# A gated recurrent mixer and its ternary FFN on one Trainium2 core: every engine's order in the mix stage is rewritten, the DMA issues of ScalarE go to SyncE and GpSimd

## The reference, cut to what matters

```
bc = einsum('bti,oi->bto', value, W_bc).reshape(B, T, H=32, 4, N=32)
bc = bc / (sqrt(sum(bc*bc, -1)) + EPS)
Bz, Bx, Cz, Cx = bc[...,0,:], bc[...,1,:], bc[...,2,:], bc[...,3,:]
def step(z, s):                      # for each of 512 positions
    S = 1 / (1 + dt*k + dt*dt*A)
    z = S * (z - dt*A*s + dt*Bz*u)
    s = s + dt*z + dt*Bx*u
    y = Cz . z + Cx . s
```

## Time and profile before

| | us |
|---|---|
| median of 3 runs | 2783.38 (2770.19 to 2786.92) |
| the profiled execution | 2786.88 |
| its span in the trace | 2785.2 |
| project / mix / ffn in the span | up to about 320 / 320 to 2466 / 2466 to 2785 |
| PE, DVE, ACT busy over the span | 81%, 67%, 42% |

### The profile page before, as it was taken

One profiled execution on the slowest core, in us unless ns is written; L12 is line 12 of the kernel. 1 busy time (PEld: TensorE's weight loads), 2 busy tenths in 40 slices (PEclk: granted clock), 3 DMA queues, 4 the chain that ended last, 5 costly groups with the idle time before them and its releaser, 6 DMA issues. The chain is left out here.

```text
span 2785.2 us, 56799 instructions
## 1 busy us (share of the span) xinstructions
PE 2266.9 (81%) x20514; PEld 1412.6 (51%) x20514; DVE 1869.4 (67%) x4268; ACT 1167.1 (42%) x2659; POOL 362.4 (13%) x540
## 2 busy tenths in 40 slices
PE   5655387989889898989898998989898997646886
PEld 2322133555555555555554555555555556545775
DVE  5655336867668776858676777668586777527775
ACT  3444233444526253534435353535445352313543
POOL 0000011111111111111111111111011110025210
PEclk9777688899889898889898898989888886557997
DMA  3444443334343434334443434243443433052320
GB/s 117 123 135 141 140 119 97 111 109 120 96 113 109 115 90 123 95 102 117 107 116 90 119 103 121 80 132 101 106 123 100 109 100 84 3 193 111 130 75 23
DMA packets 240313, 299.22 MB, mean 107 GB/s; under 512 B 127905, under 2 KB 144289, under 8 KB 231841
## 3 DMA queue, kind: packets, MB, share of 16 engines
q1 hardware_dynamic: 129248, 145.24, 17.5%
q10 hardware_dynamic: 93248, 112.51, 15.1%
q0 software_dynamic: 17536, 37.78, 5.0%
HBM read 240.85 MB, written 51.39 MB: 105 GB/s over the span
## 5 line engine op out<-in xcount | busy, mean ns | idle before, releaser
L642 PE MATMUL m_ps_a<-m_valT,m_w_bc 128*128 128x512 f32 x2048 | 1063.5, 672 | 67.0 <-DMA m_valT<-scratch_valT 32.1
L642 PEld LDWEIGHTS m_ps_a<-m_valT,m_w_bc 128*128 128x128 f32 x2048 | 426.3, 217 | 574.9 <-issue 565.4
L597 POOL DMA_DIRECT2D m_shear<-scratch_shear x512 | 277.1, 542 | 1831.5 <-DVE m_psi L1004 1617.1
L1000 DVE TENSOR_TENSOR m_prod<-m_psi,m_shear 128x128 f32<-128x128 f32 x1024 | 294.9, 288 | 38.7 <-ACT m_shear L771 14.0
L1004 DVE TENSOR_TENSOR m_psi<-m_psi,m_prod 128x128 f32<-128x128 f32 x1024 | 293.4, 287 | 17.2
L812 ACT ACTIVATE m_sq<-m_ps_a 128x512 f32<-128x512 f32 x256 | 153.2, 598 | 293.5 <-PE m_ps_a L642 235.1
L771 ACT ACTIVATE m_shear<-m_shear,m_A 128x64 f32<-128x64 f32 x512 | 135.8, 338 | 332.8 <-DMA m_shear<-scratch_shear 301.6
L698 PE MATMUL m_ps_g<-m_raw 32*64 32x64 f32 x8192 | 189.2, 253 | 69.1 <-DVE m_g L1108 61.3
L678 PEld LDWEIGHTS m_ps_k<-m_u,m_kT 64*128 64x128 f32 x1792 | 190.0, 197 | 67.7 <-ACT m_kT L838 39.7
L723 PE MATMUL m_ps_k<-m_raw,m_Xb 128*112 128x64 f32 x1024 | 177.2, 306 | 57.3 <-ACT m_Xb L856 57.3
L698 PEld LDWEIGHTS m_ps_g<-m_raw 32*64 32x64 f32 x8192 | 168.7, 163 | 96.3 <-issue 80.2
(11 more groups left out here) (146 smaller groups left out, 2975.8 us busy)
## 6 DMA issues: line engine op xcount, KB each, us to landing
m_scale<-scratch_norm SPq DMA_DIRECT2D x512, 128.0 KB
m_w_bc<-in_w_bcT ACTq DMA_DIRECT2D x252, 256.0 KB, 2.9
m_shear<-scratch_shear POOLq DMA_DIRECT2D x512, 64.0 KB, 2.7
m_det<-scratch_ab ACTq DMA_DIRECT2D x64, 256.0 KB, 5.9
scratch_gateT<-gate SPq DMA_DIRECT2D x8, 1024.0 KB, 3.9
scratch_valT<-val SPq DMA_DIRECT2D x8, 1024.0 KB, 4.5
scratch_svgT<-svg SPq DMA_DIRECT2D x8, 1024.0 KB, 5.8
scratch_u<-p_u SPq DMA_DIRECT2D x8, 1024.0 KB, 7.7
```

What stands on the lines that cost most here:

```text
L597: pool.dma_start(shear[h * N:(h + 1) * N, w % 2].rearrange("p k g t -> p k (g t)"), spread(src)).then_inc(into.sem, into.step)
L642: mm = pe.matmul(ps_a[j % 2].ap(), w_bc[:, j, kt, :], valT[:, kt, :], start=(kt == 0), stop=(kt == KI - 1))
L1000: dve.tensor_tensor(prod.ap().rearrange("p k g r -> p (k g) r"), psi_kt[of_half][:, :, t, :], window.unsqueeze(2).to_broadcast([P, 2 * HAL ...
```

## The change

- `LEAD` is 5 instead of 4: TensorE is one unit further ahead.
- TensorE, state part: before, `transposes`, unit, `state_terms`, unit, for each group (the fourth without the last unit). After, unit, `transposes`, unit, `state_terms`, so 8 units there instead of 7.
- TensorE, scores: half of a unit (two of its four weight tiles) is put behind each of the two bursts of scores, instead of a whole unit behind both. Between the outputs of a group and the scores of the next, there is one more unit; three units that stood behind the first group's scores and two that stood before the last outputs are spread out so.
- TensorE, `state_terms`: a semaphore increment on `narrow_next` ahead of it. Its matmuls stay as they are.
- ScalarE issues no more `valT`, `e_end`, `u`, `y` and `ab` DMAs. `ab` goes to GpSimd, all the others to SyncE, where a list for each half now orders them with the norm traffic. ScalarE keeps the loads of `w_bc`.
- ScalarE's order: logs of the determinants move from the start of a half to the end of the half before it, between window 9 and the third copy of `y`; the exponentials move ahead by one unit.
- VectorE's order: scaling of a group's inputs and outputs comes earlier by up to two steps, so that at the start of a half only keys are left of the current half; `queries` of the second group come before `states` (so the wait on `X_ready` goes from the second group's queries to the third's, as they share a buffer); the last mask comes before the keys of the next half instead of after it.

```diff
-    LEAD, PHASE = 4, UNITS // 2
+    LEAD, PHASE = 5, UNITS // 2
...
@@ sync
+                def norm_rows(b, group):
+                    sp.wait_ge(rows_ready.sem, rows_ready.at(b, group - 1))
+                    load_factor(b + group // HG, group % HG)
+                    compact_norms(b, group)
+                def input_scales(b, group):
+                    sp.wait_ge(rows_ready.sem, rows_ready.at(b, group))
+                    sp.dma_start(dram["norm"][group % 2]..., compact.ap()).then_inc(rows_stored.sem, rows_stored.step)
+                    sp.wait_ge(rows_stored.sem, rows_stored.at(b, group))
+                    sp.wait_ge(c_scaled.sem, c_scaled.at(b, group - 1))
+                    load_scales(group % 2, 0)
+                def output_scales(b, group):
+                    sp.wait_ge(b_scaled.sem, b_scaled.at(b, group))
+                    load_scales(group % 2, 1)
+                def store_y(b, group, more):
+                    sp.wait_ge(y_ready.sem, y_ready.at(b, group * 2 + 1))
+                    for h in range(HP):
+                        sp.dma_start(dram["yT"][b, group, h * DH:(h + 1) * DH, :],
+                                     y[h * N:h * N + DH, :]).then_inc(y_stored.sem, y_stored.step)
+                    if more:
+                        load_u(b, group + HALF)
...
+                    for half in range(2):
...
+                        if more:
+                            norm_rows(b, then)
+                            input_scales(b, then)
+                            load_e_end(b, half + 1)
+                            output_scales(b, then)
+                            norm_rows(b, then + 1)
+                            input_scales(b, then + 1)
+                            output_scales(b, then + 1)
+                            norm_rows(b, then + 2)
+                        if half == 0 and not last:
+                            sp.wait_ge(a_made.sem, a_made.at(b, UNITS - 1))
+                            load_valT(b + 1)
+                        store_y(b, first, more)
+                        if more:
+                            input_scales(b, then + 2)
+                            output_scales(b, then + 2)
+                            norm_rows(b, then + 3)
+                        store_y(b, first + 1, more)
+                        if more:
+                            input_scales(b, then + 3)
+                            output_scales(b, then + 3)
+                        store_y(b, first + 2, more)
+                        store_y(b, first + 3, more)
...
@@ gpsimd
+                            if w == NW and not (last and half):
+                                pool.wait_ge(det_used.sem, det_used.at(b, half))
+                                load_ab(b, half + 1)
...
@@ tensor
+                    pe.sem_inc(narrow_next, 1)
...
-                    product(b, unit, last)
+                        product(b, unit, last, pair * 2, pair * 2 + 2)
...
                         for i in range(HALF):
+                            products(b, unit, 1, last)
                             transposes(b, first + i)
-                            products(b, unit, 1, last)
+                            products(b, unit + 1, 1, last)
                             state_terms(b, first + i)
...
                         scores_and_unit(b, first, unit, last)
-                        products(b, unit + 1, 3, last)
+                        products(b, unit + 1, 1, last)
...
                             scores_and_unit(b, first + i, unit, last)
                             outputs(b, first + i - 1)
-                            unit += 1
-                        products(b, unit, 2, last)
-                        unit += 2
+                            products(b, unit + 1, 1, last)
+                            unit += 2
                         outputs(b, first + HALF - 1)
...
@@ scalar
                         copy_terms(b, first + 1)
+                        det_inverses(b, half)
                         evacuated(1)
...
                         block_states(b, first)
                         window(6)
                         evacuated(1)
+                        copy_y(b, first)
+                        block_states(b, first + 1)
                         window(7)
+                        evacuated(2)
                         window(8)
+                        copy_y(b, first + 1)
+                        block_states(b, first + 2)
                         evacuated(1)
                         window(9)
+                        if more:
+                            det_logs(b, half + 1)
+                        evacuated(1)
+                        copy_y(b, first + 2)
+                        block_states(b, first + 3)
+                        evacuated(1)
+                        copy_y(b, first + 3)
...
@@ vector, the order of a half after the change (then = the same group of the next half)
    keys(first+1); scales(then); keys(first+2); scale_inputs(then); det_sums; scale_outputs(then);
    keys(first+3); queries(first); queries(first+1); scales(then+1); coefficients; states; mask(first);
    scale_inputs(then+1); queries(first+2); mask(first+1); scale_outputs(then+1); scales(then+2);
    queries(first+3); scale_inputs(then+2); mask(first+2); scale_outputs(then+2); scales(then+3);
    advance(OF_PHASE); scale_inputs(then+3); mask(first+3); keys(then); scale_outputs(then+3)
```

More of the change, by code:

```diff
@@ new lines, in load_e_end, with load_u @@
+                def load_e_end(b, half):
+                    for h in range(HP):
+                        first = h * HG + half % 2 * HALF
+                        sp.dma_start(e_end[h * N:(h + 1) * N, half % 2 * HALF:half % 2 * HALF + HALF, :],
+                                       spread(dram["e_end"][b + half // 2, first:first + HALF])).then_inc(e_end_in.sem, e_end_in.step)
+                def load_u(b, group):
+                    g_ = group % HG
+                    of_group = slice(g_ * HP * DH, (g_ + 1) * HP * DH)
+                    into = u_in[group % HALF]
+                    sp.dma_start(u[:, group % HALF], dram["u"][b + group // HG][:, :, of_group]).then_inc(into.sem, into.step)
@@ new lines, in _ @@
+                load_valT(0)
+                load_e_end(0, 0)
+                for group in range(HALF):
+                    load_u(0, group)
+                for group in range(HALF):
+                    norm_rows(0, group)
+                    input_scales(0, group)
+                    output_scales(0, group)
+                def body(b, last):
+                    for half in range(2):
+                        more = not (last and half)
+                        first = half * HALF
+                        then = first + HALF
+                        if more:
[21 more added lines that the diff above has]
+                        store_y(b, first + 3, more)
@@ L587, in _, with load_ab @@
                 over_rows(sp, body)
+                sp.wait_ge(y_stored.sem, y_stored.at(B - 1, HG * HP - 1))
             @block.gpsimd
             def _(pool):
+                def load_ab(b, half):
+                    for h in range(HP):
+                        first = h * HG + half % 2 * HALF
+                        pool.dma_start(det[h * N:(h + 1) * N, :, :],
+                                       spread(dram["ab"][b + half // 2, first:first + HALF])).then_inc(ab_in.sem, ab_in.step)
@@ L807, in evacuate @@
                     act.wait_ge(a_made.sem, a_made.at(b, unit))
-                    if unit == UNITS - 1 and not last:
-                        load_valT(b + 1)
                     if j == 0 and unit:
@@ L824, in det_logs @@
                     for i in range(HALF):
-                        group = half * HALF + i
+                        group = half % 2 * HALF + i
                         ins = act.activation(det[:, i, :], det[:, i, :], ACT.Ln, bias=one[:, :], scale=A[:, group:group + 1])
@@ L881, in _ @@
                         scale_shear(0, 0, (unit + 1) // 2)
+                    if unit == 2:
+                        det_logs(0, 0)
                 scale_shear(0, 1, 0)
@@ L928, in body @@
                         copy_terms(b, first + 3)
-                        if more:
-                            load_e_end(b, half + 1)
                         window(5)
@@ L1212, in phase @@
                     queries(b, first + 3, advance)
+                    if more:
+                        scale_inputs(b, then + 2, advance)
                     mask(b, first + 2, advance)
                     if more:
-                        scale_inputs(b, then + 2, advance)
+                        scale_outputs(b, then + 2, advance)
                         scales(b, then + 3, advance)
                     advance(OF_PHASE)
-                    advance = stepping(b, half + 2, not last)
                     if more:
-                        keys(b, then, advance)
-                    if half:
-                        advance = stepping(b, half + 2, False)
```

(4 more changed lines are left out.)

116 lines of the change are left out of this document (29 added, 87 removed).

## The result

| | before | after |
|---|---|---|
| median, us | 2778.43 (2770.19 to 2786.92, 4 runs) | 2836.38 (2835.70 to 2846.56, 4 runs) |
| span of the profiled execution | 2785.2 | 2834.0 |

The changed kernel is slower: ratio 1.0209, 95% interval 1.0179 to 1.0240, 58 us. I had forecast 2748.

A forecast was written before the change was run, and what follows sets the result against it. The bound was a loop of dependences per half, T + C = 126.7 us, falling to 121.9; with valT 4 per row this saved 44, less 9 for prologue and last half: 2752 profiled, 2748 median, range 2650 to 2835.

The forecast's parts named there:

- T: Tail of the loop, from the last psi step to the next half's first `scales`: 30.6 us, forecast 29.6.
- C: Rest of the loop, from first `scales` to last psi step: 96.1 us, forecast 92.3.
- work in C: VectorE's work between first `scales` and last psi step: 73.3 us, plus 7.0 for moved keys and steps, 80.3.
- waits in C: VectorE's waits between first `scales` and last psi step: forecast 12 us per half, against 22.8.
- (d): Last part of T: y copy, SyncE's y stores and u, then factor and compact loads until landing: 10.4 us.
- the 9.65: VectorE's last listed wait in C, 9.65 us; to go, as the last compact loads follow an earlier scaling.
- valT: SyncE issues this load some 2.5 us after unit 31; TensorE waits 3 to 4: 4 per row, bounds 0 and 8.
- Row border: ScalarE's idle 8.58 us between rows: counted as nothing, or 5 per row if SyncE had such a stall.
- Prologue: Start of the kernel: 14 us longer, as the fourth group's input and output scaling precede the first keys.
- Table load: ScalarE's table switch, taken as 1.28 us without drain; the skill's 1.38 drain would make the sum 2769.
- The slower rival: SyncE becomes the bound: its waits for y copies delay third and fourth groups' scale loads; 2838 us, chance 0.21.
- Signs named beforehand: Right: compact waits from 281 to about 150 us; C wrong: `m_scale` waits far above 6 per half.

The follow-up runs named there:

- e6: Changed kernel, with ScalarE instead of SyncE issuing each half's last group's four y stores and u load: 2767.5 us.
- e2: Changed kernel, with ScalarE's logs of the next half's determinants ahead of shear window 9 instead of behind it: 2786.3 us.
- e1: Changed kernel, with GpSimd's 1 MB `ab` load held until the next half's third group's input scaling is done: 2788.0 us.
- e11: Changed kernel with the edits of e2 and e6, windows 2 and 3 behind the term copies, and the `ab` load held as in e1: 2714.6 us.
- e15: Changed kernel with the edits of e2 and e6, windows 2 and 3 behind the term copies, and ScalarE issuing `ab` ahead of window 8: 2686.3 us.
- e16: Changed kernel, with the last group's y stores and u load, and the `ab` load ahead of window 8, back on ScalarE: 2734.9 us.
- e9: Changed kernel, with whole units again three behind the first scores (one halved) and two ahead of the last outputs: 2970.9 us.
- e13: Changed kernel, with all four groups' y stores and u loads issued by ScalarE again: 2796.2 us.
- e3c: Changed kernel, with the next group's factor and compact loads ahead of SyncE's last y stores and u load, in first halves only: 2805.4 us.
- e14: Changed kernel, with shear windows 2 and 3 behind the copies of the first two groups' terms: 2839.0 us.

## Why the prediction was wrong, step by step

The two parts of the loop, averaged over 13 halves in the middle of either trace:

| | before | predicted | after |
|---|---|---|---|
| T | 31.7 | 29.6 | 30.8 |
| C | 95.6 | 92.3 | 99.3 |
| work in C | 73.5 | 80.3 | 81.0 |
| waits in C | 22.1 | 12 | 18.3 |

- **T** was sized well (1.2 off), part by part: from the last psi step to the last outputs it is 20.0 for 19.2, from there to the reciprocals 10.8 for 10.4. That last term, (d), already had SyncE's y stores and u load ahead of the next half's factors and compact loads. So the cost that e6 takes away stood in my sum. What I did not see is that it could be avoided: e2 and e6 cut T by 4.2 and 7.7.
- **Work in C** was right too: it grew by 7.5, for the 7.0 that I counted. So against the kernel before, T is 0.9 shorter and C 3.7 longer: the moved keys were to be paid for by 10 us less waiting, and the waits fell by 3.8 only.
- **The failed step is the sum of the waits in C**: 12 forecast, 18.3 measured, which over 15 halves makes 95 us, where the median lies 88 from the forecast. Those that I listed came out: input scaling 1.8 for 2.5, exponentials 2.6 for 1.5, states 3.5 for 4, output scaling of the third group 2.1 for 3.2, masks 1.2 for 0.8. Two were missing: the third group's input scaling, 5.5, and the fourth group's reciprocals, 1.8. The second is what is left of the 9.65 that was to go (9.1 on average before). The first is new: before, VectorE waited 0.1 there. The moved `ab` load had no cost in my sum at all: e1 takes the load away from these scale loads, and the wait goes to 0.9. e11, e15 and e16 show that the load's place decides what it costs.
- **valT**: SyncE issues it 2.6 us after unit 31, for the 2.5 that I took, and TensorE does wait, 2.2 on average, once per row. The halves with the wait, which also hold the row border, are only 1.9 longer than the others (131.2 and 129.3), so at most 1.9 of the 4 per row shows. Where the wait is longer it does show (e9).
- **Row border** 0: right. The gap of 11 between the two kinds of halves (before 132.8 and 121.5) has shrunk to 2: the halves with the border got 1.6 shorter, the others 7.8 longer.
- **Prologue** 14: it was 22.4. **Last half** -5: it was -10.2. Together 3 off.
- **Table load**: the row of 1.28 in the tail is followed by the first log 0.01 us later, as in the earlier trace rows. By the Trainium skill (ScalarE: Activation LUTs, What ACT_TABLE_LOAD costs) some 1.4 us of drain would stand beside it; this trace again has no room for that.
- **narrow_next** 0: not tried alone.
- The slower rival had the time, 2838, and the sign, late scale loads. It had the cause wrong: not SyncE's waits for the first two y copies ahead of the scale loads (e13 leaves those waits nearly as they were), but GpSimd's load beside them (e1). That its number was met is luck.
- With the two transfers put back the change gives 2735 (e16), 13 from my forecast. That is luck as well: T is 23.6 there for my 29.6 and C 98.6 for my 92.3, and the two errors cancel.
- Signs named beforehand: waits for `m_scale` far above 6 per half were to show C wrong. Those in C are 9.5 per half (1.8, 5.5 and 2.1), and with the 6.4 of the fourth group in the tail about 16. The compact waits fell to 188 and not to 150.

What stays open: why the units' new placement costs the kernel before 54 us, of which its `valT` waits, 2.6 per row, are at most 18 (TensorE's list and ScalarE's fixed list may not fit each other, which was only argued); why e1 gained most of its time in the tail; and what the 3 of 7 us are made of that came back in C in e3c.

## What to carry to other kernels

When a transfer changes its queue, price two things besides its issue: what is queued behind it at that moment (3.5 us of stores and a load ahead of seven small loads cost 69 us here), and which small latency-bound loads it will share the DMA engines with (1 MB ahead of 512 KB cost 48 in one version of this kernel, 33 and 18 in others). Moving a wait's cause shows its worth only when the next wait in the loop is named: e14 and e11 removed a wait and gained nothing. And the order of one engine is not a free choice when the others' orders are fixed: the same placement of units cost 54 us in the kernel before, and its undoing 135 in the changed one.

## What was not expected of the hardware

- A single u load took SyncE 1.52 us to issue (1261.30), and 0.63 elsewhere (1367.62 in the same trace). Every u load in the loop stands behind four y stores; most take 0.55 to 0.65, and 9 of 56 take 1.0 to 1.8. Why is not shown.
- With one 1 MB load beside them, four scale loads of 128 KB were through 9.0 us after the first issue (after), and at most 5.0 us without it (e1).
